# A two-layer transformer block on Trainium2: the value products of an item put in one stretch, the turned probabilities written over the probabilities

## The chip, the cores and the metric

The kernel runs on one core of one Trainium2 chip. The metric is the device time of one execution in microseconds; the median of several runs is compared. The core has a matrix engine (PE, TensorE), a vector engine (DVE), an activation engine (ACT), a general engine (POOL, GpSimd) and a queue that issues transfers (SP). Each engine runs its own list of instructions in order, and engines wait for each other by semaphores that count upwards. Matrix products land in PSUM, eight banks of 128 partitions x 512 words, called `pb[:, bank]`.

## What is computed

Sixteen sequences of 256 tokens and 256 channels. A cross attention comes first; behind it stand two layers, in which nearly all of the time goes. One layer, cut to what matters here:

```python
def _layer(x, ...):
    qkv = shift_token(x) @ wqkv
    q, k, v = split(qkv)                      # 8 heads of 64
    q, k = l2norm(q) * qs, l2norm(k) * ksc
    q, k = rotary_xpos(q, k)
    sim = q @ k.T                             # window: own block of 128 tokens and the one before
    attn = softmax(mask(sim))
    x = x + (attn @ v) @ wo
    h = layernorm(shift_token(x)) * lg + lb
    a, g = split(h @ w1 + b1)
    x = x + (a * gelu(g)) @ w2 + b2
```

## The kernel before

One sequence in one layer is an item; there are 2 x 16 = 32. The layers are a pipeline of four items: in each pass of `run_l` the kernel projects item a, does the attention of item b, the first half of the feed-forward of item c (`hidden`) and its second half of item d (`feed`). The order of work on every engine is written out by hand in that engine's `run_l`, and nothing reorders it. Layers are run with plain passes at their ends and a hardware loop of two items per round in the middle.

The attention of an item is cut into six units, each a tile of 128 rows x 512 columns. Units 0 to 3 hold two heads each for the second block of queries (256 keys), units 4 and 5 hold four heads each for the first block (128 keys). For each unit:

- PE makes the scores in bank 3 or 4 (`scores`, line 825), two units at a time.
- DVE adds the mask, takes the row's maximum and writes the scores to `p_t[:, u]` (`maxes`, line 1596).
- ACT takes the exponential in place and sums it (`exps`, line 1222).
- DVE takes the inverse of the sums and scales `p_t[:, u]` (`norm_probs`, line 1610).
- PE turns (transposes) `p_t[:, u]` in four pieces into the unit's bank (`turn_p`, line 840; `PT_BANK` is 5, 7, 5, 7, 5, 2).
- ACT copies the bank to `pt_t[:, u % 4]` (`probs_copy`, line 1213). `pt_t` has four places for six units, so the copies of units 4, 0 and 2 wait until products that read the place are done (`pe_av`).
- PE multiplies values with turned probabilities (`weigh`, line 856), 16 products for each pair of units j = 0, 1, 2, into banks 6 and 7.

ACT then rounds the result to `o_hi` (`out_hi`, line 1229), DVE takes the rest to `o_lo` (`out_lo`, line 1640), and PE multiplies by the output weights (`out_product`, line 894).

PE's order from the middle of a pass on is: `feed` 5 of item d (line 880), `turn_h`, the last projection (line 567), `turn_p` 1 and 2, the turn of the next x (line 581), `weigh` j = 0, `turn_p` 3, `hidden` 0, `turn_p` 4, `hidden` 1 and 2, `turn_p` 5, `weigh` j = 1 and 2, `hidden` 3 and 4, `out_product` half 0, `hidden` 5, the turns of queries and keys (line 920), `out_product` half 1. The products of `hidden` and of the projections all have line 567, that of the helper `split_product`.

In the same stretch DVE's order is: the scaling of unit 3, the residual of item d (`second_residual`, line 1634, which waits for `feed` 5), the inverse sums of unit 4, the clamp of the squared norms of half 0 (line 1567), the scaling of unit 4, two roundings for `hidden`, the maxima of unit 5, the rotation of half 1 (lines 1577 and 1583), its squares (line 1562), the inverse sums of unit 5, the clamp of half 1, the scaling of unit 5, and the low part of the next x (line 1347). POOL raises the clamped norms to the power -1/2 (line 1823), adds the two parts of the rotation (line 1828) and scales them (line 1835), first for half 0, then for half 1. ACT's order is: copies 1 and 2, the exponentials of unit 5, copies 3 and 4, the rounding of the next x (line 1170), the copy of values (line 1182), GELU of chunk 0 (line 1201), in some passes a rounding of weights (`next_weights`, line 1040), copy 5, GELU of chunk 1, `out_hi`.

Other waits that are named below: `turn_p` 3 waits until copy 1 has left bank 7, `turn_p` 4 until copy 2 has left bank 5; `hidden` 0 waits for the maxima of unit 5, which free bank 4; `hidden` 1 waits for the rotation of half 1, which frees bank 0.

Of the kernel before, what the change touches and what calls it, by code (L numbers as in the profile page):

```python
# [22 lines left out]
ACT = mybir.ActivationFunctionType  # L23
AX = mybir.AxisListType

P = 128
SEQS, T, D = 16, 256, 256
NT = T // P
KC = D // P
HEADS, DH = 8, 64  # L30
# [17 lines left out]
UNITS = 6  # L48
# [40 lines left out]
def at(n, per, k):  # L89


    if isinstance(n, int):
        return n * per + k
    i, c = n
    return i * (2 * per) + (c * per + k)
# [7 lines left out]
def plus(n, d):  # L103
    return n + d if isinstance(n, int) else (n[0], n[1] + d)
# [6 lines left out]
def later(n):  # L111

    return not (isinstance(n, int) and n == 0)


def build(nc, x, ctx_in, xwq, xwk, xwv, xwo, xbo, wqkv, qsc, ksc, wo, lng, lnb, w1, b1, w2, b2, rope, mask, ident, out):
    ctx = ExitStack()
    with ctx:
        def sb(name, shape, dt=F32, where=ctx):
            return where.enter_context(nc.sbuf_tensor(name, shape, dt))  # L120

        def sem(name):
            return ctx.enter_context(nc.semaphore(name))
# [5 lines left out]
        pb = ctx.enter_context(nc.psum_tensor("pb", [P, 8, 512], F32))  # L129
# [70 lines left out]
        L = ctx.enter_context(ExitStack())  # L200
# [5 lines left out]
        qk_t = sb("qk_t", [P, 2, IC, T], where=L)  # L206
        v_t = sb("v_t", [P, 2, NT, INNER], where=L)
        p_t = sb("p_t", [P, UNITS, 512], where=L)
        pt_t = sb("pt_t", [P, 4, 512], where=L)
        s_nm = sb("s_nm", [P, UNITS, 4], where=L)  # L210
        s_sum = sb("s_sum", [P, UNITS, 4], where=L)
        s_inv = sb("s_inv", [P, UNITS, 4], where=L)
# [58 lines left out]
        pe_qkv, act_sq, act_v = sem("pe_qkv"), sem("act_sq"), sem("act_v")  # L271
# [4 lines left out]
        pe_pt, act_pt, pe_av, act_ohi, dve_olo = sem("pe_pt"), sem("act_pt"), sem("pe_av"), sem("act_ohi"), sem("dve_olo")  # L276
        pe_wo, dve_x1, pool_x1b = sem("pe_wo"), sem("dve_x1"), sem("pool_x1b")
# [46 lines left out]
        def l_roles(g):  # L324

            a = g if not isinstance(g, int) or g < ITEMS else None
            b = plus(g, -1) if not isinstance(g, int) or 1 <= g <= ITEMS else None
            c = plus(g, -2) if not isinstance(g, int) or 2 <= g <= ITEMS + 1 else None
            d = plus(g, -3) if not isinstance(g, int) or g >= 3 else None
            return a, b, c, d, (g if isinstance(g, int) else g[1]) % 2  # L330
# [26 lines left out]
        PT_BANK = [5, 7, 5, 7, 5, 2]  # L357
# [13 lines left out]
        def heads_of(u):  # L371

            return range(u // 2 * 4 + u % 2, u // 2 * 4 + 4, 2) if u < 4 else range(u % 2, HEADS, 2)
# [185 lines left out]
        def _(pe):  # L559
# [270 lines left out]
            def turn_p(a, b, d, u):  # L830

                pe.wait_ge(dve_pn, at(b, UNITS, u + 1))
                if u == 1 and d is not None:
                    pe.wait_ge(dve_x2, at(d, 1, 1))
                if 2 <= u < 5:
                    pe.wait_ge(act_pt, at(b, UNITS, u - 1))
                if u == 5 and a is not None:
                    pe.wait_ge(act_v, at(a, NT, NT))
                for k in range(4):
                    mm = pe.transpose(pb[:, PT_BANK[u], k * P:k * P + P], p_t[:, u, k * P:k * P + P], id_f)  # L840
                mm.then_inc(pe_pt, 1)

            def weigh(b, c, par, j):

                pe.wait_ge(act_pt, at(b, UNITS, 2 * j + 2))
                if j == 0:
                    pe.wait_ge(act_v, at(b, NT, NT))
                    if c is not None:
                        pe.wait_ge(dve_x1, at(c, 1, 1))
                for k in range(2 if j < 2 else 4):  # L850
                    for t in range(NT if j < 2 else 1):
                        for u in (2 * j, 2 * j + 1):
                            h = heads_of(u)[k]
                            r, col = (h % 2) * DH, (h // 2 % 2) * T + (P if j < 2 else 0)
                            piece = 2 * k + t if j < 2 else k
                            mm = pe.matmul(pb[r:r + DH, 6 + h // 4, col:col + P], v_t[:, par, t, h * DH:h * DH + DH],  # L856
                                           pt_t[:, u % 4, piece * P:piece * P + P],
                                           start=(t == 0), stop=(t == NT - 1 or j == 2))
                mm.then_inc(pe_av, 1)

            def feed(c, d, k):
# [62 lines left out]
            def run_l(g, layer=None):  # L924
                a, b, c, d, par = l_roles(g)
# [60 lines left out]
                    idle_products(42, 7)  # L986
                    pe.wait_ge(x_res1, SEQS)
                if b is not None:
                    weigh(b, c, 1 - par, 0)
                    turn_p(a, b, d, 3)  # L990
                if c is not None and not last_attention:
                    hidden(a, b, c, 0)
# [9 lines left out]
                    hidden(a, b, c, 0)  # L1002
                if b is not None:
                    turn_p(a, b, d, 5)
                    weigh(b, c, 1 - par, 1)
                    weigh(b, c, 1 - par, 2)
                if c is not None and not last_attention:
                    hidden(a, b, c, 3)
                    hidden(a, b, c, 4)
# [21 lines left out]

            x_iterations(run_x)
            l_iterations(pe, run_l, between)


        @block.scalar
        def _(act):
# [168 lines left out]

            def probs_copy(b, u):
                act.wait_ge(pe_pt, at(b, UNITS, u + 1))
                if u == 4:
                    act.wait_ge(pe_av, at(b, 3, 1))  # L1210
                elif u in (0, 2) and later(b):
                    act.wait_ge(pe_av, at(plus(b, -1), 3, 3 if u == 0 else 2))
                nc.scalar.activation(pt_t[:, u % 4], pb[:, PT_BANK[u]], ACT.Copy).then_inc(act_pt, 1)  # L1213

            def exps(b, j):

# [7 lines left out]
                e.then_inc(act_exp, 1)  # L1224

            def out_hi(b):
                act.wait_ge(pe_av, at(b, 3, 3))
                for k in range(2):
                    nc.scalar.activation(o_hi[:, 2 * k:2 * k + 2].rearrange("p c t -> p (c t)"), pb[:, 6 + k],
                                         ACT.Copy).then_inc(act_ohi, 1)  # L1230
# [19 lines left out]
            def run_l(g, layer=None):  # L1250
# [11 lines left out]
                if b is not None:  # L1262
                    exps(b, 3)
                    probs_copy(b, 0)
                    exps(b, 4)
# [4 lines left out]
                if b is not None:  # L1270
                    probs_copy(b, 1)
                if a is not None and not is_first(a):
                    square(a, 1, 1)
                if b is not None:
                    probs_copy(b, 2)
                    exps(b, 5)
                    probs_copy(b, 3)
                    probs_copy(b, 4)
# [4 lines left out]
                if last_attention:  # L1283
                    probs_copy(b, 5)
                    out_hi(b)
# [12 lines left out]
                if b is not None and not last_attention:  # L1298
                    out_hi(b)
# [30 lines left out]
        def _(dve):  # L1330
# [255 lines left out]
            def maxes(b, j):  # L1586

                heads = 2 if j < 4 else 4
                keys = 512 // heads
                m = mask_t[:].rearrange("p a n -> p (a n)")[:, 2 * P - keys:]  # L1590
                dve.wait_ge(pe_s, at(b, UNITS, j + 1))
                if later(b):
                    dve.wait_ge(pe_pt, at(plus(b, -1), UNITS, j + 1))
                dve.sem_inc(scores_seen, 1)
                for k in range(heads):
                    e = nc.vector.tensor_tensor_reduce(p_t[:, j, k * keys:k * keys + keys],  # L1596
                                                       pb[:, S_BANK[j], k * keys:k * keys + keys], m, -1.0, FAR, ALU.add,
                                                       ALU.min, s_nm[:, j, k:k + 1])
                e.then_inc(dve_max, 1)
# [69 lines left out]
            def run_l(g, layer=None):  # L1669
# [11 lines left out]
                if b is not None:  # L1681
                    maxes(b, 0)
                    maxes(b, 1)
# [4 lines left out]
                if b is not None:  # L1688
                    maxes(b, 2)
                    maxes(b, 3)  # L1690
# [282 lines left out]
```

## Time and profile before

| | us |
|---|---|
| median of 3 runs | 1419.7 (1419.18 to 1420.46) |
| span of the profiled execution, first to last instruction | 1416.2 |
| PE busy | 1385.3 |
| DVE busy | 1090.6 |
| ACT busy | 935.8 |
| POOL busy | 761.9 |

The profile is of one execution. All times of instructions are microseconds from the start of its span. A timeline row gives the start, the time taken, the engine, the line, the operation, what is written <- what is read, the shape and how many are merged in the row; in brackets stands how long the engine was idle before it and what ended that. Ends of matrix products are modelled and overlap with the next ones, so the distance from one start to the next tells more than the time taken. PEld is the load of the stationary operand.

### The profile page before, as it was taken

The numbers are of one execution on the slowest core, as the hardware profiler recorded it, in microseconds if no ns is written. First come the engines' busy times: TensorE is split into PE (matmuls) and PEld (weight loads), VectorE is DVE, ScalarE is ACT, GpSimd is POOL, SyncE is SP. The second block draws the span as 40 slices with busy tenths as digits, with TensorE's granted clock in tenths as the row PEclk, the third lists the DMA queues.
The fourth block names the chain that finished last, engine by engine and source line by source line (L and its number), as shares of the span: only waits on it lengthen the run. The fifth ranks groups of instructions, "written<-read, shape, count | busy, mean of one in ns | idle before, by whom it ended". The sixth has DMA issues, their size and how long they took to land.

```text
span 1416.2 us, 32735 instructions
## 1 busy us (share of the span) xinstructions
PE 1385.3 (98%) x11563; PEld 1237.8 (87%) x11563; DVE 1090.6 (77%) x3067; ACT 935.8 (66%) x2662; POOL 761.9 (54%) x576
## 2 busy tenths in 40 slices
PE   8999999989999999999999999999999999999998
PEld 7999998778888888888888888888888888888887
DVE  5777776768788788888888878778778888888874
ACT  6877777456666666666666667666666666666662
POOL 1212222556566566666666667666656666666653
PEclk9999999999999999999999999999999999999999
DMA  5223122101100100010001211111111111111001
GB/s 190 90 92 110 48 67 90 47 20 29 30 30 30 30 29 28 28 28 28 28 29 29 71 29 37 33 35 37 37 37 37 36 36 36 36 36 37 29 30 31
DMA packets 50516, 63.41 MB, mean 45 GB/s; under 512 B 8402, under 2 KB 32104, under 8 KB 50408
## 3 DMA queue, kind: packets, MB, share of 16 engines
q1 hardware_dynamic: 50408, 61.99, 14.0%
q8 instruction: 65, 1.06, 0.3%
q14 instruction: 43, 0.35, 0.1%
HBM read 38.17 MB, written 16.78 MB: 39 GB/s over the span
## 4 chain that ended last, share of the span: by engine, by line
PE 65%; DVE 16%; ACT 9%; issue 5%; DMA 2%; POOL 1%; SPq 1%; DVEq 0%; ACTq 0%; POOLq 0%
PE pb L567 30%; PE pb L880 6%; PE pb L894 6%; PE pb L856 5%; PE pb L825 5%; PE pb L840 5%; ACT x_p L1079 4%; PE pb L920 4%; DVE p_t L1596 2%; DVE p_t L1610 2%; ACT x_pt L1085 2%; DVE r_sin L1583 2%; DVE n_sq L1562 2%; DMA x<-x 1%; DVE r_cos L1577 1%
## 5 line engine op out<-in xcount | busy, mean ns | idle before, releaser
L1823 POOL TENSOR_TENSOR n_inv<-n_cl,half_neg 128x16 f32<-128x16 f32 x64 | 211.2, 3299 | 178.2 <-DVE n_cl L1567 174.7
L1222 ACT ACTIVATE p_t<-p_t,s_nm 128x128 f32<-128x128 f32 (+1 forms) x512 | 227.0, 447 | 22.3 <-DVE s_nm L1596 20.9
L567 PE MATMUL pb<-h_hi,w_hi 128*128 128x256 f32 x704 | 207.5, 295 | 1.3 <-DVE h_lo L1558 1.2
L567 PE MATMUL pb<-h_hi,w_lo 128*128 128x256 f32 x704 | 198.7, 282 | 0.0
L567 PE MATMUL pb<-h_lo,w_hi 128*128 128x256 f32 x704 | 198.6, 282 | 0.0
L1828 POOL TENSOR_TENSOR r_cos<-r_cos,r_sin 128x1024 f32<-128x1024 f32 x64 | 154.6, 2415 | 53.8 <-DVE r_sin L1583 53.8
L1213 ACT ACTIVATE pt_t<-pb 128x512 f32<-128x512 f32 x192 | 114.3, 597 | 98.5 <-PE pb L840 97.8
L1178 ACT ACTIVATE qk_sq<-pb 128x512 f32<-128x512 f32 x128 | 72.5, 592 | 142.9 <-PE pb L567 141.5
L567 PE MATMUL pb<-wqkv_hi,xt_hi 128*128 128x512 f32 x384 | 163.9, 427 | 2.6 <-DVE r_sin L1583 2.3
L1859 POOL TENSOR_TENSOR hg_lo<-hg,hg_hi 128x256 fp32r<-128x256 f32 (+1 forms) x192 | 141.9, 760 | 44.5 <-DVE hg_hi L1627 44.5
L1596 DVE CUSTOM_DVE_ANT_0 p_t<-pb,mask_t 128x128 f32<-128x128 f32 (+1 forms) x512 | 151.9, 353 | 17.5 <-PE pb L825 17.3
L567 PE MATMUL pb<-wqkv_lo,xt_hi 128*128 128x512 f32 x384 | 152.0, 396 | 0.0
L567 PE MATMUL pb<-wqkv_hi,xt_lo 128*128 128x512 f32 x384 | 150.8, 393 | 0.0
L567 PEld LDWEIGHTS pb<-h_hi,w_hi 128*128 128x128 f32 x704 | 134.0, 190 | 8.3 <-issue 6.9
L567 PEld LDWEIGHTS pb<-h_lo,w_hi 128*128 128x128 f32 x704 | 134.5, 191 | 0.0
L567 PEld LDWEIGHTS pb<-h_hi,w_lo 128*128 128x128 f32 x704 | 134.1, 191 | 0.0
L1610 DVE TENSOR_TENSOR p_t<-p_t,s_inv 128x512 f32<-128x512 f32 x192 | 129.3, 687 | 0.1
L1835 POOL TENSOR_TENSOR r_cos<-r_cos,n_inv 128x1024 f32<-128x1024 f32 x64 | 122.0, 1907 | 5.0
L840 PE MATMUL pb<-ones_at,p_t 128*128 128x128 f32 x768 | 115.0, 279 | 5.0 <-DVE p_t L1610 4.0
L825 PE MATMUL pb<-qk_t 64*128 64x128 f32 (+1 forms) x1024 | 109.8, 343 | 1.0 <-DVE s_nm L1596 0.6
L1620 DVE SCALAR_TENSOR_TENSOR hg<-pb,b_t,gl 128x256 f32<-128x256 f32 (+1 forms) x192 | 86.4, 475 | 31.0 <-ACT gl L1203 19.0
L1079 ACT ACTIVATE x_p<-pb,x_nm 128x77 f32<-128x77 f32 x256 | 79.2, 338 | 42.9 <-DVE x_nm L1374 42.9
(145 smaller groups left out, 3907.5 us busy)
## 6 DMA issues: line engine op xcount, KB each, us to landing
y_state<-x SPq DMA_DIRECT2D x32, 256.0 KB, 2.0
x_cur<-y_state SPq DMA_DIRECT2D x32, 256.0 KB, 2.6
x_res<-y_state SPq DMA_DIRECT2D x32, 256.0 KB, 2.8
x_in<-x SPq DMA_DIRECT2D x16, 256.0 KB, 2.9
x_state<-x SPq DMA_DIRECT2D x16, 256.0 KB, 2.0
x_orig<-x_state SPq DMA_DIRECT2D x16, 256.0 KB, 2.9
out<-x SPq DMA_DIRECT2D x16, 256.0 KB, 2.2
x<-x SPq DMA_DIRECT2D x32, 112.0 KB, 2.3
```

The lines of the kernel that those rows point to most:

```text
L567: mm = pe.matmul(dst, s, m, start=(n == 0 and k == 0), stop=(n == len(pairs) - 1 and k == 2))
L825: mm = pe.matmul(pb[:, S_BANK[u], k * keys:k * keys + keys], qk_t[r:r + DH, 0, ch, q_cols], qk_t[r:r + DH, 1, ch, 0:keys], start=True, sto ...
L840: mm = pe.transpose(pb[:, PT_BANK[u], k * P:k * P + P], p_t[:, u, k * P:k * P + P], id_f)
L1079: e = nc.scalar.activation(x_p[:, u, k, :], pb[:, 2 + u % 2, k * P:k * P + CTX], ACT.Exp, bias=x_nm[:, u, k:k + 1], scale=1.0, accum_out=x ...
L1213: nc.scalar.activation(pt_t[:, u % 4], pb[:, PT_BANK[u]], ACT.Copy).then_inc(act_pt, 1)
L1222: e = nc.scalar.activation(pu, pu, ACT.Exp, bias=s_nm[:, j, k:k + 1], scale=-1.0, accum_out=s_sum[:, j, k:k + 1])
L1596: e = nc.vector.tensor_tensor_reduce(p_t[:, j, k * keys:k * keys + keys], pb[:, S_BANK[j], k * keys:k * keys + keys], m, -1.0, FAR, ALU.ad ...
L1610: nc.vector.tensor_tensor(pu, pu, s_inv[:, u, 0:heads].unsqueeze(2).broadcast_to([P, heads, 512 // heads]), ALU.mult).then_inc(dve_pn, 1)
L1823: nc.gpsimd.tensor_tensor(n_inv[:, t], n_cl[:, t], half_neg[:], ALU.pow).then_inc(pool_inv, 1)
L1828: nc.gpsimd.tensor_tensor(r_cos[:, t], r_cos[:, t], r_sin[:, t], ALU.add).then_inc(pool_sum, 1)
L1835: nc.gpsimd.tensor_tensor(rows, rows, n_inv[:, t].unsqueeze(2).broadcast_to([P, 2 * HEADS, DH]), ALU.mult).then_inc(pool_qk, 1)
L1859: nc.gpsimd.tensor_tensor(hg_lo[0:rows, m], hg[0:rows, m], hg_hi[0:rows, m].bitcast(F32), ALU.subtract).then_inc(pool_hglo, 1)
```

## The change

The buffer `pt_t` is removed. The copies of the turned probabilities go back into `p_t[:, u]`, from which they were turned, one place for each of the six units. With six places the three waits of the copies for `pe_av` are dropped. The three calls of `weigh` become one, behind the turn of unit 5, with a single wait for the copies of all six units; the 16 products of j = 0 so move from behind the turn of x to that place. `pe_av` now counts once per item instead of three times. The maxima of the next item, which write `p_t` again, wait for the value products of the item before instead of for its turns.

```diff
-        pt_t = sb("pt_t", [P, 4, 512], where=L)
...
-            def weigh(b, c, par, j):
-
-                pe.wait_ge(act_pt, at(b, UNITS, 2 * j + 2))
-                if j == 0:
-                    pe.wait_ge(act_v, at(b, NT, NT))
-                    if c is not None:
-                        pe.wait_ge(dve_x1, at(c, 1, 1))
-                for k in range(2 if j < 2 else 4):
-                    for t in range(NT if j < 2 else 1):
-                        for u in (2 * j, 2 * j + 1):
...
-                                           pt_t[:, u % 4, piece * P:piece * P + P],
-                                           start=(t == 0), stop=(t == NT - 1 or j == 2))
+            def weigh(b, c, par):
+
+                pe.wait_ge(act_pt, at(b, UNITS, UNITS))
+                pe.wait_ge(act_v, at(b, NT, NT))
+                if c is not None:
+                    pe.wait_ge(dve_x1, at(c, 1, 1))
+                for j in range(3):
+                    for k in range(2 if j < 2 else 4):
+                        for t in range(NT if j < 2 else 1):
+                            for u in (2 * j, 2 * j + 1):
...
+                                               p_t[:, u, piece * P:piece * P + P],
+                                               start=(t == 0), stop=(t == NT - 1 or j == 2))
                 mm.then_inc(pe_av, 1)
...
                 if b is not None:
-                    weigh(b, c, 1 - par, 0)
                     turn_p(a, b, d, 3)
...
                     turn_p(a, b, d, 5)
-                    weigh(b, c, 1 - par, 1)
-                    weigh(b, c, 1 - par, 2)
+                    weigh(b, c, 1 - par)
...
             def probs_copy(b, u):
                 act.wait_ge(pe_pt, at(b, UNITS, u + 1))
-                if u == 4:
-                    act.wait_ge(pe_av, at(b, 3, 1))
-                elif u in (0, 2) and later(b):
-                    act.wait_ge(pe_av, at(plus(b, -1), 3, 3 if u == 0 else 2))
-                nc.scalar.activation(pt_t[:, u % 4], pb[:, PT_BANK[u]], ACT.Copy).then_inc(act_pt, 1)
+                nc.scalar.activation(p_t[:, u], pb[:, PT_BANK[u]], ACT.Copy).then_inc(act_pt, 1)
...
             def out_hi(b):
-                act.wait_ge(pe_av, at(b, 3, 3))
+                act.wait_ge(pe_av, at(b, 1, 1))
...
                 if later(b):
-                    dve.wait_ge(pe_pt, at(plus(b, -1), UNITS, j + 1))
+                    dve.wait_ge(pe_av, at(plus(b, -1), 1, 1))
```

## Rows read from the trace of the kernel before

**Rows 1.** The page: busy time and share of the span; granted clock in 40 slices.
```profile
PE 1385.3 (98%) x11563; PEld 1237.8 (87%) x11563; DVE 1090.6 (77%) x3067; ACT 935.8 (66%) x2662; POOL 761.9 (54%) x576
...
PEclk9999999999999999999999999999999999999999
```
**Rows 2.** Stretches: length, then busy us of each engine, clock, DMA share, GB/s.
```profile
420.00:695.00 275.00, 274.68 (x2227) 245.35 (x2226) 219.86 (x622) 181.26 (x471) 171.18 (x120) 1.00 0.10 29
```
**Rows 3.** Waits, 380 to 1360 us: who <- whom: total us, times, longest.
```profile
DVE o_lo L1640 <- ACT o_hi L1229: 61.2, 28, 3.2
...
PEld pb L567 <- issue: 22.7, 82, 0.3
...
DVE x L1634 <- PE pb L880: 10.8, 22, 0.6
...
PEld pb L856 <- ACT pt_t L1213: 7.3, 30, 0.9
```
**Rows 4.** Timeline of PE, 699 to 713 us, one item.
```profile
699.84 0.40 PE L880 MATMUL pb<-w_hi,hg_hi 128*128 128x256 f32 x2
...
703.31 1.09 PE L856 MATMUL pb<-pt_t,v_t 128*64 128x128 f32 x16
704.34 0.66 PE L840 MATMUL pb<-ones_at,p_t 128*128 128x128 f32 x4
...
706.26 0.60 PE L840 MATMUL pb<-ones_at,p_t 128*128 128x128 f32 x4
706.61 0.36 PE L567 MATMUL pb<-h_hi,w_hi 128*128 128x256 f32 x1
...
709.67 0.66 PE L840 MATMUL pb<-ones_at,p_t 128*128 128x128 f32 x4
710.26 1.97 PE L856 MATMUL pb<-pt_t,v_t 128*64 128x128 f32 x32
712.16 0.38 PE L567 MATMUL pb<-h_hi,w_hi 128*128 128x256 f32 x1
```
**Rows 5.** Timeline of DVE, same item.
```profile
700.37 0.69 DVE L1634 TENSOR_TENSOR x<-pb,x1b 128x512 f32<-128x512 f32 x1 [0.60 <-PE pb L880]
...
701.06 0.14 DVE L1567 TENSOR_SCALAR n_cl<-n_sq 128x16 f32<-128x16 f32 x1
...
704.91 1.28 DVE L1583 TENSOR_TENSOR r_sin<-pb,sin_t 128x512 f32<-128x512 f32 x2
...
707.35 1.67 DVE L1567 TENSOR_SCALAR n_cl<-n_sq 128x16 f32<-128x16 f32 x1
708.94 0.68 DVE L1610 TENSOR_TENSOR p_t<-p_t,s_inv 128x512 f32<-128x512 f32 x1
```
**Rows 6.** Timeline of POOL, same item.
```profile
701.28 3.36 POOL L1823 TENSOR_TENSOR n_inv<-n_cl,half_neg 128x16 f32<-128x16 f32 x1 [5.70 <-DVE n_cl L1567]
...
706.59 2.41 POOL L1828 TENSOR_TENSOR r_cos<-r_cos,r_sin 128x1024 f32<-128x1024 f32 x1
```
**Rows 7.** Timeline of PE: the turn of unit 5, first and last item.
```profile
284.65 0.66 PE L840 MATMUL pb<-ones_at,p_t 128*128 128x128 f32 x4 [0.40 <-DVE p_t L1610]
...
1380.48 0.66 PE L840 MATMUL pb<-ones_at,p_t 128*128 128x128 f32 x4 [0.87 <-DVE p_t L1610]
```
**Rows 8.** Timeline of ACT, the item of rows 4.
```profile
709.86 0.47 ACT L1201 ACTIVATE gl<-pb,b_t 128x256 f32<-128x256 f32 x1
710.37 0.60 ACT L1213 ACTIVATE pt_t<-pb 128x512 f32<-128x512 f32 x1
```
**Rows 9.** Timeline of PE and ACT, an item in which ACT rounds weights.
```profile
888.57 0.66 PE L840 MATMUL pb<-ones_at,p_t 128*128 128x128 f32 x4
...
890.30 0.59 ACT L1213 ACTIVATE pt_t<-pb 128x512 f32<-128x512 f32 x1
...
890.94 1.09 PE L856 MATMUL pb<-pt_t,v_t 128*64 128x128 f32 x16 [0.68 <-ACT pt_t L1213]
```
**Rows 10.** A stretch with long pauses of PE; columns as in rows 2.
```profile
1391.00:1400.00 9.00, 5.84 (x46) 5.28 (x45) 7.16 (x16) 1.97 (x4) 4.67 (x7) 1.00 0.11 34
```

More of the change, by code:

```diff
@@ L841, in turn_p @@
                 mm.then_inc(pe_pt, 1)
-            def weigh(b, c, par, j):
-                pe.wait_ge(act_pt, at(b, UNITS, 2 * j + 2))
-                if j == 0:
-                    pe.wait_ge(act_v, at(b, NT, NT))
-                    if c is not None:
-                        pe.wait_ge(dve_x1, at(c, 1, 1))
-                for k in range(2 if j < 2 else 4):
-                    for t in range(NT if j < 2 else 1):
-                        for u in (2 * j, 2 * j + 1):
[L853 to L856, printed above, removed]
-                                           pt_t[:, u % 4, piece * P:piece * P + P],
-                                           start=(t == 0), stop=(t == NT - 1 or j == 2))
+            def weigh(b, c, par):
[7 more added lines that the diff above has]
+                            for u in (2 * j, 2 * j + 1):
+                                h = heads_of(u)[k]
+                                r, col = (h % 2) * DH, (h // 2 % 2) * T + (P if j < 2 else 0)
+                                piece = 2 * k + t if j < 2 else k
+                                mm = pe.matmul(pb[r:r + DH, 6 + h // 4, col:col + P], v_t[:, par, t, h * DH:h * DH + DH],
+                                               p_t[:, u, piece * P:piece * P + P],
+                                               start=(t == 0), stop=(t == NT - 1 or j == 2))
                 mm.then_inc(pe_av, 1)
```

## Prediction

> **What bounds the kernel now.** I read the page's busy shares first, then the busy time by stretches, then the list of waits, and last one item of the steady part in order of time on every engine. PE is busy 98% of the span at a granted clock of 1.00 in all slices [rows 1], and in the steady part 274.68 of 275.00 us [rows 2]. So the kernel is PE's instruction stream, one item about every 35.3 us, and any pause put into that stream is paid in full unless PE was already pausing there. The list of waits [rows 3] shows what the other engines do: DVE stands still for `o_hi` in 28 of 28 items, so it starts the second half of each item from the end of the value products. That is 61.2 us of DVE waiting that costs nothing today, but it says that a later end of the value products shifts the rest of the item.
>
> Second view: PE in the item whose value products start at 703.31 [rows 4]. The last product of `feed` 5 starts at 699.84 (a pair), the first value stretch of 16 runs from 703.31 to 704.34, unit 4 is turned at 706.26, `hidden` 1 and 2 fill 706.61 to at most 709.67, unit 5 is turned at 709.67, and the other 32 value products run from 710.26 to 712.16.
>
> Third view: DVE and POOL in the same stretch [rows 5, 6]. DVE adds the residual `x2` at 700.37, released by the last `feed` product, and clamps half 0 at 701.06. POOL raises that to a power from 701.28 (3.36 us), scales, and adds the rotated parts of half 1 from 706.59 to 709.00. DVE's clamp of half 1 starts at 707.35 and ends only at 709.02; its twin at 701.06 took 0.14 us. Then the probabilities of unit 5 are scaled from 708.94 to 709.62, and PE turns them at 709.67, 0.05 us later. This is a second chain, as long as PE's own work in the same stretch: from the last `feed` product to the turn of unit 5 it passes through no value product. In all 32 items the turn of unit 5 starts 0.05 us behind the end of that scaling; the first and the last of the 32 stand in [rows 7].
>
> The rule that bears on the long clamp is in the Trainium skill, page "SBUF — State Buffer", section "Who interferes with whom": a DVE instruction in a two-port mode, tensor_scalar among them, and a GpSimd instruction take one port pair as a lock, and the one that comes second blocks for the whole of the other. By that rule the trace agrees (1.67 against 0.14 us, and it ends with POOL's add). By the rule the chain is as fixed as POOL's instructions and the sum below stands at +50.7; if the clamp could slip by, it would be the +40 of the rival "the chain is shorter".
>
> **The change, part by part.**
> 1. The first 16 value products leave their place behind the turn of `x`. That takes 704.34 − 703.31 = 1.03 us out of PE's stream between `feed` 5 and the turn of unit 5 [rows 4]. It is no gain, since the turn of unit 5 is released by DVE at 709.62 whatever PE does before. PE only arrives early: `hidden` 1 has to wait for the rotation, which ends at 704.91 + 1.28 = 706.19 [rows 5] (two instructions with that sum), and `hidden` 1 and 2 take at most 709.67 − 706.61 = 3.06 us, so PE stands at unit 5 by 709.30 and waits 0.37 us or more; the rest of the 1.03 us is waited ahead of `hidden` 0 and 1. Gain taken: 0. Bounds: 0 to 1.03 us per item.
> 2. All value products now wait for the copy of unit 5. Before, the 16 of j = 1 needed only units 2 and 3 and covered that copy. The copy starts 710.37 − 709.67 = 0.70 us after the turn starts and takes 0.60 us [rows 4, 8]. From copy to product I take 0.05 us: in the one item of [rows 9] where the products did wait for this copy, it ends at 890.30 + 0.59 = 890.89 and they start at 890.94. So the stretch starts 0.70 + 0.60 + 0.05 = 1.35 us after the turn, where it started 0.59 us after it. Queued behind this wait on PE are the value products, `hidden` 3 to 5, `out_product` and the next item's scores; ACT (`out_hi`) and DVE (`out_lo`) wait for the products.
> 3. The stretch is 48 products instead of 32. Sixteen take 1.03 us with the change to another kind of product behind them, 32 take 1.90, so 16 more add 0.87: 2.77 us [rows 4]. Bounds: 3 × 0.87 = 2.61 and 1.90 + 1.03 = 2.93.
> 4. End of the stretch after the turn of unit 5: 1.35 + 2.77 = 4.12 us, before 712.16 − 709.67 = 2.49. **Per item +1.63 us** (1.47 to 1.79 by the bounds of step 3).
> 5. ACT is not late for the copy: before, GELU of chunk 0 ends at 709.86 + 0.47 = 710.33 and the copy starts at 710.37 [rows 8], with no room left. But GELU needs `hidden` 0, which now ends earlier (no 16 products ahead of it), and so do the copies 3 and 4. If ACT did not come earlier, the copy would start where it did. Cost 0.
> 6. In two items, those where ACT also rounds the next layer's weights ahead of this copy, the copy was late already: the turn is at 888.57, the copy at 890.30 instead of 889.27 [rows 9]. There the old stretch had already split. If the copy comes no earlier the item pays 2.77 − 1.03 = 1.74 us; if it comes on time, 1.03 us less. I take +0.9 each.
> 7. The copies write into `p_t` instead of `pt_t`. The form is the same, 128×512 out of PSUM; no row shows this target for it, and the 0.60 us of [rows 8] is kept (below it the 0.59 of [rows 9], nothing above). Three waits of the copies on `pe_av` go; they name products that PE had passed before the turns they follow, and each copy is behind a turn anyway. DVE's maxima wait for `pe_av` of the item before instead of `pe_pt`; PE runs those products ahead of the scores the same instruction waits for, so it costs 0, and behind it nothing is held.
> 8. Behind the stretch nothing takes the shift up: DVE, ACT and PE all continue from its end, and DVE's 61.2 us of waiting for `o_hi` [rows 3] grow. Only POOL and the DMAs come earlier relative to it, and PE waits for them next to never.
>
> Sum: 30 × 1.63 + 2 × 0.9 = 50.7 us. The profiled execution has a span of 1416.2 us and the median of the runs is 1419.7, so 3.5 us lie around the span and are kept: 1416.2 + 50.7 + 3.5 = **1470.4 us**, 3.6% slower.
>
> **The rivals.**
> - *The chain slides along.* If what releases unit 5 hung on PE's place in the stream and not on `feed` 5, the turn would come 1.03 us earlier and the item would pay 1.63 − 1.03 = 0.60 us: 32 × 0.60 = +19, 1439 us. For it: in some items DVE does not wait for `feed` 5 (22 of 28 do [rows 3]). Against: everything DVE and POOL do between the two, from 700.37 to 709.62, reads no value product [rows 5, 6].
> - *The chain is shorter.* If the clamp of half 1 were not held until POOL's add ends, scaling could be done 1.5 us earlier and PE's own arrival, 0.37 us earlier than now, would rule: 1.63 − 0.37 = 1.26 us, 32 times: +40, 1460 us. Against: POOL's add starts at 706.59, before the clamp at 707.35, and nothing in the change moves either.
> - *The clock falls.* Each item gets pauses of some 0.4 us and 0.76 us on both sides of four transposes. If the clock went from 2.4 to 1.2 GHz for the value products, they would take another 2.77 us: 32 × 2.77 = 89 more, 1559 us. Against: in the nine microseconds of [rows 10] PE was busy only 5.84 us and the granted clock stayed 1.00. Beside it stands the Trainium skill, page "TensorE: Matmul & The Clock Gate", section "A second HAM failure mode: psum-queue depth-cycling", which tells of a kernel whose small pauses between groups let the clock swing; [rows 10] do not agree with it here.
> - *PE's own pauses vanish: not slower.* Each item gets 1.63 us longer for everything that is not on the chain, so pauses that PE makes elsewhere could close. The largest are 22.7 us ahead of the products of line 567, 82 times, and 7.3 us for these copies; the other entries are under 5 us each [rows 3]. The kernel is not slower from the point where 50.7 us of pauses close, which is nearly all of them. Against: the 22.7 us have no releaser and look like the change from one kind of product to another, of which the new order drops one or two per item and counts in step 3.
>
> **How the numbers follow.** Forecast 0.84, chain slides 0.05, chain shorter 0.05, clock 0.03, pauses vanish 0.03 (half of it no difference, half a gain). The forecast's own range: the low bound of step 3 gives 30 × 1.47 + 1.4 = 45.5, less up to 0.6 us in the items with irregular waits, some 4 us: 1461. The high bound gives 30 × 1.79 + 2 × 1.74 = 57: 1477. With the "shorter" case at its lower edge the range 1460 to 1477 holds about 8 in 10. This kernel's runs tell a difference of about 0.2% from none. Slower 0.97, the same 0.015, faster 0.015.
>
> **What would show it right or wrong.** After: the turn of unit 5 again 0.05 us behind DVE's scaling in all items, now with PE pauses ahead of it (about 1 us per item, at `hidden` 0, `hidden` 1 and the turn); the copy 0.70 us behind the turn; one stretch of 48 products starting 1.35 us after the turn and ending at 4.12; the item 36.9 us long. It is wrong if the time from `feed` 5 to that turn falls below 9.3 us, if the copy starts later than 0.7 us after the turn (ACT late), or if the granted clock shows less than 1.00.

## The result, and the profile after

| | before | after |
|---|---|---|
| median us (lowest to highest) | 1419.44 (1415.61 to 1420.46, 4 runs) | 1466.84 (1466.51 to 1467.3, 4 runs) |
| span of the profiled execution | 1416.2 | 1464.8 |
| PE busy | 1385.3 | 1395.2 |
| DVE busy | 1090.6 | 1076.9 |
| POOL busy | 761.9 | 760.6 |

The ratio is 1.0342, with a 95% interval of 1.0327 to 1.0356: 47.4 us slower, against 51 forecast; the span grew by 48.6.

The page of the changed kernel: busy time, and the granted clock in 40 slices. They answer to [rows 1].

```profile
PE 1395.2 (95%) x11563; PEld 1239.2 (85%) x11563; DVE 1076.9 (74%) x3067; ACT 935.4 (64%) x2662; POOL 760.6 (52%) x576
...
PEclk9999999999999999999999999999999999999999
```

The same number of instructions on every engine, the same clock, and a share of PE that fell by three points: nearly all of the loss is pauses, not work. (PE's busy time is 9.9 us longer with the same products; the ends of its records are modelled.) A stretch of the steady part as long as the one of [rows 2] (length, then busy us of PE, PEld, DVE, ACT, POOL, clock):

```profile
437.00:712.00 275.00, 265.01 (x2105) 234.27 (x2104) 205.83 (x599) 171.01 (x445) 157.41 (x114) 1.00 0.10 28
```

PE was busy 274.68 of 275 us before and is busy 265.01 now. In 275 us there are 275 / 36.9 = 7.5 items, so the records show 9.67 / 7.5 = 1.3 us more of pause per item (ends of matrix products are modelled, so a short pause is partly covered). Where they sit is in the list of waits of the changed kernel, 395 to 1406 us, again 28 items (who <- whom: total us, times, longest); it answers to [rows 3]:

```profile
DVE o_lo L1633 <- ACT o_hi L1222: 110.9, 28, 4.5
...
PEld pb L855 <- ACT p_t L1206: 25.4, 27, 1.4
...
PE pb L855 <- ACT p_t L1206: 19.0, 27, 1.1
...
PEld pb L566 <- DVE r_sin L1576: 14.1, 29, 1.2
...
PEld pb L839 <- DVE p_t L1603: 11.7, 27, 0.5
```

The value products now wait for a copy in 27 items (19.0 us in which PE stands still, 0.70 us each). The products of `hidden` (line 566) wait for the rotation, and the turn of unit 5 (line 839) waits for DVE's scaling; in the rows of PEld it is the load of their stationary operand that waits. DVE's wait for `o_hi` grew from 61.2 to 110.9 us, 1.8 us more per item: the other engines were shifted with PE, and in this steady part they took up next to nothing.

One item in order of time, PE first (start, time taken). It is the item that answers to [rows 4].

```profile
720.74 0.60 PE L580 MATMUL pb<-ones_at,x_cur 128*128 128x128 f32 x4
721.25 0.63 PE L839 MATMUL pb<-ones_at,p_t 128*128 128x128 f32 x4
...
721.82 0.39 PE L566 MATMUL pb<-h_hi,w_hi 128*128 128x256 f32 x1
...
723.34 0.60 PE L839 MATMUL pb<-ones_at,p_t 128*128 128x128 f32 x4
724.21 0.39 PE L566 MATMUL pb<-h_hi,w_hi 128*128 128x256 f32 x1 [0.27 <-DVE r_sin L1576]
727.61 0.66 PE L839 MATMUL pb<-ones_at,p_t 128*128 128x128 f32 x4 [0.26 <-DVE p_t L1603]
728.95 2.84 PE L855 MATMUL pb<-p_t,v_t 128*64 128x128 f32 x48 [0.69 <-ACT p_t L1206]
731.73 0.39 PE L566 MATMUL pb<-h_hi,w_hi 128*128 128x256 f32 x1
```

DVE, POOL and ACT in the same item answer to [rows 5, 6, 8].

```profile
718.31 0.69 DVE L1627 TENSOR_TENSOR x<-pb,x1b 128x512 f32<-128x512 f32 x1 [0.57 <-PE pb L879]
...
725.32 1.65 DVE L1560 TENSOR_SCALAR n_cl<-n_sq 128x16 f32<-128x16 f32 x1
726.88 0.68 DVE L1603 TENSOR_TENSOR p_t<-p_t,s_inv 128x512 f32<-128x512 f32 x1
```

```profile
724.53 2.39 POOL L1821 TENSOR_TENSOR r_cos<-r_cos,r_sin 128x1024 f32<-128x1024 f32 x1
```

```profile
726.87 0.47 ACT L1198 ACTIVATE gl<-pb,b_t 128x256 f32<-128x256 f32 x1
728.30 0.60 ACT L1206 ACTIVATE p_t<-pb 128x512 f32<-128x512 f32 x1 [0.97 <-PE pb L839]
```

From DVE's residual to the turn of unit 5 it is 727.61 − 718.31 = 9.30 us, as before (709.67 − 700.37 = 9.30, [rows 4, 5]), though PE has 1.03 us less to do in between. From the turn it is 1.34 us to the stretch and 4.12 us to its end (731.73 − 727.61), against 2.49 before. ACT stood idle for 0.97 us before the copy, so ACT is not late. This item is 36.9 us long where it was 35.3.

### The profile page after: what moved, and what is told of

It reads as the page before. It is cut to its first block, busy times and chain, and to the rows that moved or that the text cites. A ratio compares the mean times of both kernels' runs of the same rounds, so it can differ in the third digit from the quotient of the medians.

```text
span 1464.8 us, 32641 instructions
## 1 busy us (share of the span) xinstructions
PE 1395.2 (95%) x11563; PEld 1239.2 (85%) x11563; DVE 1076.9 (74%) x3067; ACT 935.4 (64%) x2662; POOL 760.6 (52%) x576
## 4 chain that ended last, share of the span: by engine, by line
PE 44%; DVE 29%; ACT 12%; issue 9%; DMA 3%; SPq 2%; DVEq 0%; POOL 0%; ACTq 0%; POOLq 0%
PE pb L566 17%; PE pb L855 6%; PE pb L893 6%; DVE p_t L1589 4%; PE pb L879 4%; ACT x_p L1076 4%; DVE n_sq L1555 4%; DVE p_t L1603 4%; PE pb L919 4%; DVE r_cos L1570 3%; PE pb L824 3%; DVE r_sin L1576 3%; DMA x<-x 2%; ACT p_t L1215 2%; SPq L521 2%
## 5 line engine op out<-in xcount | busy, mean ns | idle before, releaser
L1206 ACT ACTIVATE p_t<-pb 128x512 f32<-128x512 f32 x192 | 113.2, 596 | 98.3 <-PE pb L839 96.2
L1633 DVE TENSOR_TENSOR o_lo<-pb,o_hi 128x512 fp32r<-128x512 f32 x64 | 43.8, 687 | 128.0 <-ACT o_hi L1222 128.0
L839 PEld LDWEIGHTS pb<-ones_at,p_t 128*128 128x128 f32 x768 | 84.7, 140 | 32.8 <-DVE p_t L1603 19.1
```

What stands on the lines that cost most here:

```text
L1206: nc.scalar.activation(p_t[:, u], pb[:, PT_BANK[u]], ACT.Copy).then_inc(act_pt, 1)
```

## The experiments

**The buffer alone.** The copies go to `p_t` and the maxima wait for `pe_av`; three calls and places of `weigh` as before.

```diff
-                                           pt_t[:, u % 4, piece * P:piece * P + P],
+                                           p_t[:, u, piece * P:piece * P + P],
...
-                nc.scalar.activation(pt_t[:, u % 4], pb[:, PT_BANK[u]], ACT.Copy).then_inc(act_pt, 1)
+                nc.scalar.activation(p_t[:, u], pb[:, PT_BANK[u]], ACT.Copy).then_inc(act_pt, 1)
...
-                    dve.wait_ge(pe_pt, at(plus(b, -1), UNITS, j + 1))
+                    dve.wait_ge(pe_av, at(plus(b, -1), 3, j // 2 + 1))
```

> The kernel before with the buffer part of the change alone: the copies go into p_t, the maxima wait for pe_av of the item before, and weigh keeps its three calls and its three places. My theory: the buffer costs nothing, the time is that of the kernel before, 1419 us within 2. Rival (the new target of the copies, or the maxima's new wait, carries part of the loss): from 1425 us up, and copies longer than 0.60 us.

Measured: 1416.73 us against 1417.56 of the kernel before, run again beside it, ratio 0.9995 (0.9985 to 1.0004). The group of the copies in its trace (busy, mean ns | idle before):

```profile
L1208 ACT ACTIVATE p_t<-pb 128x512 f32<-128x512 f32 x192 | 114.3, 597 | 99.5 <-PE pb L839 97.7
```

114.3 us and 597 ns; the group of `pt_t` in the kernel before has the same two numbers. The buffer, the copies' target and the maxima's wait for `pe_av` cost nothing; the whole loss lies in the order of the products and in what they wait for. (In the change the maxima wait for the last value product of the item before. PE runs it ahead of the scores for which the same instruction waits, so that this stricter form costs nothing either follows from the order and was not run by itself.)

**The move alone.** The changed kernel, but the stretch waits for two copies at a time.

```diff
-                pe.wait_ge(act_pt, at(b, UNITS, UNITS))
+                pe.wait_ge(act_pt, at(b, UNITS, 2))
...
                 for j in range(3):
+                    if j:
+                        pe.wait_ge(act_pt, at(b, UNITS, 2 * j + 2))
```

> The changed kernel, but the one stretch of 48 behind the turn of unit 5 waits for two copies at a time, as before, so it starts 0.59 us after the turn and units 0 to 3 cover the copy of unit 5. Theory 'the turn of unit 5 is held by DVE's chain': the move alone costs the 16 products in full, end of the stretch 0.59 + 2.77 = 3.36 to 3.41 us after the turn, +0.9 us per item, 1445 to 1449 us. Rival 'the turn slides forward as its 16 products leave': the move is free and the whole loss is the wait for the copy, 1416 to 1424 us here.

Measured: 1441.78 us, ratio 1.0172 (1.0155 to 1.0189), +24.2 us. PE, the same item:

```profile
718.60 0.66 PE L839 MATMUL pb<-ones_at,p_t 128*128 128x128 f32 x4 [0.28 <-DVE p_t L1605]
719.19 2.84 PE L857 MATMUL pb<-p_t,v_t 128*64 128x128 f32 x48
...
721.96 0.39 PE L566 MATMUL pb<-h_hi,w_hi 128*128 128x256 f32 x1
```

The stretch starts 0.59 us after the turn and ends 3.36 us after it, so the 16 products that were moved are paid with 0.87 us each time; the turn still waits for DVE. The rival in which the turn slides forward asked for no loss at all here and falls. The total lies 3 us under the expected 1445 to 1449. Some 2 us of this are the kernel before, which took 1417.56 us in the runs made beside this one and 1419.44 in the first ones; the rest are items that paid less than 0.87 us: the first paid nothing, and one with weights to round and one with a late transfer paid 0.04 and 0.16 us.

**The wait alone.** The 16 products of j = 0 back in their place, the other 32 behind the turn of unit 5 and waiting for its copy (copies in `p_t`).

```diff
-                pe.wait_ge(act_pt, at(b, UNITS, 2 * j + 2))
+                pe.wait_ge(act_pt, at(b, UNITS, 2 if j == 0 else UNITS))
```

> The other half: copies in p_t, the 16 products of j = 0 back behind the turn of x, and the 32 of j = 1 and 2 behind the turn of unit 5 waiting for the copy of unit 5. Theory: only the uncovered copy is paid, start at 1.35 and end at 1.35 + 1.90 = 3.25 us after the turn against 2.49, +0.76 us per item, 1441 to 1444 us; together with the run that keeps the waits staggered it adds up to the change's +47. Rival (the turn slides, the wait is the whole loss): 1464 to 1468 us. Third possibility (the two parts overlap): the two runs add up to clearly more than 47 us over the kernel before.

Measured: 1440.27 us, ratio 1.0164 (1.0147 to 1.0181), +22.7 us. PE:

```profile
716.88 0.66 PE L839 MATMUL pb<-ones_at,p_t 128*128 128x128 f32 x4
718.22 1.97 PE L855 MATMUL pb<-p_t,v_t 128*64 128x128 f32 x32 [0.69 <-ACT p_t L1208]
...
720.12 0.39 PE L566 MATMUL pb<-h_hi,w_hi 128*128 128x256 f32 x1
```

Start 1.34, end 3.24 us after the turn, 0.75 us later than before. Move and wait together are 24.2 + 22.7 = 46.9 us; the change cost 47.4. Each of the two parts is known to some 2.4 us. In the item they are 0.87 + 0.75 = 1.62 us, against 4.12 − 2.49 = 1.63. The two parts add up and do not overlap.

**What holds the turn of unit 5.** The changed kernel, with DVE's scaling of unit 5 right behind the rotation.

```diff
                     rotate(a, 1, layer)
-                    squares(a, 1)
                 if b is not None:
                     inverse_sums(b, 5)
+                    norm_probs(b, 5)
                 if a is not None and not is_first(a):
+                    squares(a, 1)
                     clamp(a, 1)
-                if b is not None:
-                    norm_probs(b, 5)
```

> The changed kernel, with DVE's inverse sums and scaling of unit 5 moved ahead of the squares and the clamp of half 1, right behind the rotation; nothing else. It takes the long clamp out of the chain ahead of the turn. Theory: the turn of unit 5 then comes as soon as PE reaches it, 0.37 to 0.47 us earlier, and the item pays 1.63 - 0.4 us: 1452 to 1456 us, with PE's remaining pause at hidden 1 (rotation). Rival (the turn was held by something else, e.g. by ACT or the rotation of half 1 alone): 1464 to 1468 us. The squares, the clamp and POOL's power come 0.7 us later; if PE waits for POOL at the turns of queries, the gain is smaller.

Measured: 1454.28 us, ratio 1.0262 (1.0244 to 1.0279): 12.6 us less than the change. PE:

```profile
718.90 0.39 PE L566 MATMUL pb<-h_hi,w_hi 128*128 128x256 f32 x1 [0.26 <-DVE r_sin L1576]
721.88 0.60 PE L839 MATMUL pb<-ones_at,p_t 128*128 128x128 f32 x4
723.16 2.84 PE L855 MATMUL pb<-p_t,v_t 128*64 128x128 f32 x48 [0.69 <-ACT p_t L1206]
```

The pause at the turn is gone and the one at `hidden` 1 stays: it was DVE's scaling, queued behind the squares and the long clamp, that held the turn. 12.6 us over 32 items are 0.39 us each; the item shown is 36.4 us long instead of 36.9, 0.47 us less, and the items with weights did not get shorter. That fits the 0.37 or more that the prediction's step 1 worked out for PE's arrival.

**Who holds the clamp.** The changed kernel, scaling ahead of the clamp but behind the squares, so that it is issued while POOL adds.

```diff
                     squares(a, 1)
                 if b is not None:
                     inverse_sums(b, 5)
+                    norm_probs(b, 5)
                 if a is not None and not is_first(a):
                     clamp(a, 1)
-                if b is not None:
-                    norm_probs(b, 5)
```

> The changed kernel, with DVE's scaling of unit 5 ahead of the clamp of half 1 only, behind the squares. The scaling has two SBUF inputs; POOL's add, which reads SBUF, is under way then. Theory after the Trainium skill, page 'SBUF - State Buffer', section 'Who interferes with whom': a DVE instruction with two SBUF inputs contends with a GpSimd instruction that reads SBUF, so now the scaling itself is held until POOL's add ends. By that rule it takes some 2.2 us instead of 0.68 and the time stays 1466 us within 2. Rival (only the clamp is held by POOL, the scaling is not): scaling done 1.5 us earlier, the turn when PE gets there, 1452 to 1456 us.

Measured: 1466.45 us, ratio 1.0334 (1.0318 to 1.035), the time of the change. DVE and POOL:

```profile
578.21 2.08 DVE L1603 TENSOR_TENSOR p_t<-p_t,s_inv 128x512 f32<-128x512 f32 x1
580.22 0.16 DVE L1560 TENSOR_SCALAR n_cl<-n_sq 128x16 f32<-128x16 f32 x1
...
577.34 2.40 POOL L1820 TENSOR_TENSOR r_cos<-r_cos,r_sin 128x1024 f32<-128x1024 f32 x1
```

Now the scaling takes 2.08 us instead of 0.68: POOL's add ends at 579.74, the scaling at 580.29, 0.55 us behind it, as if it had run only then. The clamp behind it takes 0.16 us instead of 1.65. So the wait is not a property of the clamp: whichever of the two DVE instructions comes first while POOL adds is held by that add. The Trainium skill, page "SBUF — State Buffer", section "Who interferes with whom", says in one clause that a DVE instruction in a two-port mode contends with GpSimd, and in another that a DVE instruction with two SBUF inputs contends with a GpSimd instruction that reads SBUF. The trace agrees with both by the two times; in which mode the clamp ran, no row shows.

**The same edit in the kernel before.** DVE's scaling of unit 5 behind the rotation; the diff is that of "What holds the turn", in the kernel before.

> The kernel before, with DVE's scaling of unit 5 right behind the rotation of half 1. Theory 'PE's stream is the bound of the kernel before and its pause at the turn of unit 5 is what DVE's chain leaves it': the pause there is 0.1 us in most items and 0.4 us in some, so 3 to 6 us come off: 1413 to 1417 us. Rival (DVE's chain and PE only tie, the squares, clamp and POOL's power, 0.7 us later, hold the turns of queries instead): 1419 to 1423 us.

Measured: 1413.17 us against 1418.31, ratio 0.9954 (0.994 to 0.9968): 5.1 us faster than the kernel before, the best of all versions. DVE, POOL and PE:

```profile
704.20 0.86 DVE L1610 TENSOR_TENSOR p_t<-p_t,s_inv 128x512 f32<-128x512 f32 x1
704.99 1.21 DVE L1562 TENSOR_REDUCE n_sq<-qk_sq 128x16 f32<-128x1024 f32 x1
706.23 1.13 DVE L1567 TENSOR_SCALAR n_cl<-n_sq 128x16 f32<-128x16 f32 x1
...
704.47 2.85 POOL L1827 TENSOR_TENSOR r_cos<-r_cos,r_sin 128x1024 f32<-128x1024 f32 x1
```

```profile
707.46 0.60 PE L840 MATMUL pb<-ones_at,p_t 128*128 128x128 f32 x4
707.99 1.97 PE L856 MATMUL pb<-pt_t,v_t 128*64 128x128 f32 x32
```

The scaled unit 5 lies ready 2.4 us ahead of its turn (704.20 + 0.86 against 707.46), and PE runs through. Even the kernel before was held there a little in nearly every item: the item shown is 35.14 us long here and was 35.25.

**One stretch, with its costs covered.** The changed kernel with early scaling, unit 5 turned ahead of `hidden` 2, and on ACT the copy of values ahead of the rounding of the next x.

```diff
                     hidden(a, b, c, 1)
+                    turn_p(a, b, d, 5)
                     hidden(a, b, c, 2)
...
-                    turn_p(a, b, d, 5)
+                    if c is None or last_attention:
+                        turn_p(a, b, d, 5)
                     weigh(b, c, 1 - par)
```

> The changed kernel's single stretch of 48, with its two costs covered: scaling of unit 5 early as in the run that moves it behind the rotation, the turn of unit 5 ahead of hidden 2 instead of behind it, and the copy of the values ahead of the rounding of x on ACT so that bank 2 is free. Theory: the copy of unit 5 is done under hidden 2, no pause ahead of the stretch; what is left is that PE runs 16 products less ahead of hidden 1, which waits for the rotation: some 0.4 to 0.6 us per item over the kernel before, 1430 to 1440 us. Rival (ACT cannot take the copy before GELU 0 and its table load are over, so the pause stays): 1450 to 1456 us.

Measured: 1437.89 us, ratio 1.0132 (1.0116 to 1.0148). ACT and PE:

```profile
714.87 1.28 ACT L1200 ACT_TABLE_LOAD   x1
716.16 0.47 ACT L1200 ACTIVATE gl<-pb,b_t 128x256 f32<-128x256 f32 x1
716.53 0.59 ACT L1208 ACTIVATE p_t<-pb 128x512 f32<-128x512 f32 x1
```

```profile
715.02 0.60 PE L839 MATMUL pb<-ones_at,p_t 128*128 128x128 f32 x4
717.18 2.84 PE L855 MATMUL pb<-p_t,v_t 128*64 128x128 f32 x48
```

It stands 19.6 us over the kernel before, run beside it (1418.31), so some 28 us of the 47 come back. The copy now stands behind GELU 0 and the load of its table, which alone takes 1.28 us, and starts 1.51 us after the turn; it ends at 717.12 and the stretch starts 0.06 us later, so a part of the rival was true as well. The last run takes that away.

**The copy ahead of GELU 0.** The kernel of the run "One stretch, with its costs covered", and in addition on ACT:

```diff
+                if b is not None and not last_attention:
+                    probs_copy(b, 5)
                 if c is not None:
                     gelu(c, 0, layer)
                     next_weights(g, 0)
-                if b is not None and not last_attention:
-                    probs_copy(b, 5)
```

> As the run in which unit 5 is turned ahead of hidden 2, and in addition ACT takes the copy of unit 5 ahead of GELU 0 and its table load. In that run the copy started 1.5 us after the turn, behind GELU 0, and the stretch 2.2 us after it. Theory: the copy now starts 0.7 us after the turn and is over before hidden 2 ends; the stretch starts at the end of hidden 2, 1.85 us after the turn, 0.3 us earlier per item, 1427 to 1431 us; what then stays over the kernel before is the pause at hidden 1 that the missing 16 products leave. Rival (GELU 0 is late then and DVE's gates hold PE at hidden 4): no gain, 1436 to 1440 us.

Measured: 1430.06 us, ratio 1.0077 (1.006 to 1.0094). PE:

```profile
708.53 0.60 PE L580 MATMUL pb<-ones_at,x_cur 128*128 128x128 f32 x4
...
712.00 0.38 PE L566 MATMUL pb<-h_hi,w_hi 128*128 128x256 f32 x1 [0.27 <-DVE r_sin L1578]
713.53 0.60 PE L839 MATMUL pb<-ones_at,p_t 128*128 128x128 f32 x4
715.49 2.84 PE L855 MATMUL pb<-p_t,v_t 128*64 128x128 f32 x48
718.26 0.39 PE L566 MATMUL pb<-h_hi,w_hi 128*128 128x256 f32 x1
```

No pause ahead of the stretch is left; the one ahead of `hidden` 1 is. With the copy fully hidden, the single stretch still costs 11.5 us over the kernel before. But this kernel also has the early scaling, which by itself gave the kernel before 5.1 us. Its fair partner is the run "The same edit in the kernel before", and over that one the single stretch costs 11.5 + 5.1 = 16.6 us. The same item there, on PE:

```profile
700.67 0.60 PE L581 MATMUL pb<-ones_at,x_cur 128*128 128x128 f32 x4
...
704.50 0.36 PE L567 MATMUL pb<-h_hi,w_hi 128*128 128x256 f32 x1
...
709.89 0.39 PE L567 MATMUL pb<-h_hi,w_hi 128*128 128x256 f32 x1
```

From the turn of x to `hidden` 1 it is 704.50 − 700.67 = 3.83 us with the 16 products in between and 712.00 − 708.53 = 3.47 without them. Taking out 1.03 us of products has shortened this part by 0.36 only; the other 0.67 us are waited ahead of `hidden` 0 and 1, mostly at `hidden` 1, for the rotation. From there to the end of the stretch it is 709.89 − 704.50 = 5.39 us and 718.26 − 712.00 = 6.26: the moved products cost 0.87. So the item must get 0.87 − 0.36 = 0.51 us longer, and it is 35.69 us long instead of 35.14. That is nearly the whole price of the single stretch once its copy and its turn are covered: 16 products that used to fill the time until the rotation is done have nothing in their place.

## Why the prediction was right, point by point

- **The bound.** PE's stream is the bound: in the steady part every pause in it was paid, and DVE, ACT and POOL grew only in waiting. Shown by the list of waits and by the busy share.
- **Step 1, the moved products gain nothing.** Right: the turn of unit 5 starts 0.05 us behind DVE's scaling in all 32 items after as before, and in the item shown the chain ahead of it is 9.30 us long in both. "The move alone" shows the cost, 0.87 us per item in the item shown, and the early scaling shows what held the turn. PE's pauses sit where they were forecast, at `hidden` 1 (0.27 us), at the turn (0.26 us) and, in 10 of 28 items by the records, at `hidden` 0. The 0.26 us are less than the forecast 0.37 because the modelled ends cover a part: by the starts it is 727.61 − 724.21 = 3.40 us from `hidden` 1 to the turn, where it is 707.46 − 704.50 = 2.96 in the kernel before with early scaling, so PE is held for 0.44 us.
- **Step 2, the uncovered copy.** Forecast start 1.35 us after the turn, measured 1.34.
- **Step 3, the stretch of 48.** Forecast 2.77 us, measured 731.73 − 728.95 = 2.78.
- **Step 4, +1.63 us per item.** Measured 4.12 against 2.49: 1.63.
- **Step 5, ACT.** Right: GELU 0 ends at 727.34, 0.97 us before the copy.
- **Step 6, the two items with weights.** Taken at +0.9; they paid about 0.9 and 1.1 us. In one of them the copy was still late, 1.13 us after the turn instead of 1.73.
- **Step 7, the buffer.** 0 forecast, 0.9995 measured.
- **Step 8, nothing takes it up.** Right in the steady part, wrong in the first item, which took up all of its 1.63 us. It has no `hidden` products, and PE waited for POOL in its pass, ahead of the turns of queries and keys, which the prediction had put at next to never. The row of the kernel before:

```profile
291.72 1.97 PE L920 MATMUL pb<-ones_at,r_cos 128*128 128x128 f32 x16 [1.42 <-POOL r_cos L1835]
```

After the change PE comes to this place later and does not wait. Four other items in which DVE waited 0.2 to 0.7 us less for the transfer of the shifted rows took up 0.2 to 0.6 us each. One item paid 1.1 us more than its share, since DVE waited 3.5 us for the shifted rows there instead of 2.4. That excess is no part of the change: in the run "Who holds the clamp" the same item waited 1.9 us and was 37.2 us long instead of 38.9.

The sum was 50.7 us, the span grew by 48.6. Two terms make up more than this difference. The first item's 1.6 us is one. The other is luck of one execution: in the execution after, the first turn of probabilities in the layers starts at 273.42 us, in the one before it started at 274.44, 1.02 us later. Nothing that was changed runs ahead of it, and in the ten traces of this case it starts anywhere between 273.2 and 276.5 us. The remaining items paid 0.5 us more than forecast in all, the late transfer included: 50.7 − 1.6 − 1.0 + 0.5 = 48.6.

The forecast was high by 1470.4 − 1466.84 = 3.6 us. Besides the 2.1 us of the sum, the other 1.5 us is the term around the span: I took 3.5 us, the median of the runs less the span of one profiled execution; after the change the same difference is 1466.84 − 1464.8 = 2.0. In every execution for which time and span are both known they lie 1.8 to 2.4 us apart. So the 3.5 us very likely held more than 1 us by which that execution was faster than the median; its own time is not known.

Of the rivals, "the chain slides along" fell with "The move alone". "The chain is shorter" had its mechanism right but not its condition: made true by hand, it gave 1454.28, +36.7 on the kernel before, run beside it (the rival's price was +40). The clock stayed at its upper level, 2.4 GHz: the mean granted clock of the execution is 1.00 and every slice shows a 9, with pauses of about 0.2 and 0.69 us close together in every steady item. "PE's own pauses vanish" was worth some 3 us in all, 1.6 in the first item and 1.4 in the four with the shorter transfers.

## What to carry to other kernels

Work that is taken from ahead of a waiting instruction is a gain only if nothing else sets when that instruction may run: look for the instruction that starts a constant 0.05 us behind another engine in every item, and treat what stands ahead of it on the saturated engine as free filler and what stands behind it as paid in full. When results are collected for one long stretch, the last one loses the cover that the others gave it; here turn, copy and restart exposed 1.34 − 0.59 = 0.75 us per item, nearly as much again as the lost filler. A chain that ties with the bound is worth shortening before the order of the bound is touched: one DVE scaling (with the small inverse that it needs) moved ahead of the squares and the clamp took off 0.5% (5.1 us), where the merged stretch lost 3.4%.

## What the runs showed of the hardware that I had not expected

- The stall of DVE behind POOL shows as a long instruction, not as idle time: 1.65 us for a clamp of 128×16 elements that takes 0.14 to 0.16 while POOL is not adding, 2.08 for a scaling that takes 0.68, and it passed from one to the other when their order was changed.
- Where the scaling starts shortly ahead of POOL's add, as in the runs with early scaling, it runs through with little loss (0.86 us instead of 0.68). Now POOL's add is the longer one, 2.85 us instead of 2.41, and the clamp, which still meets the add, takes 1.13 us and ends with it.
- The load of the table ahead of GELU took 1.28 us on ACT. In "One stretch, with its costs covered" it stood between the turn and its copy, and moving the copy ahead of it gave some 8 us.
- The wait for a transfer of shifted rows in one and the same item differed between the executions of three kernels, 1.9, 2.4 and 3.5 us. Two of these kernels, those with 1.9 and 3.5 us, differ only in the place of one scaling, and that item's length moved by 1.7 us between them.
